# Two halves of the scores swapped at two of seven windows, and a filter stage on quarters of the TensorE array

## The reference, cut to what matters

```python
x = x + conv_ref(_ln_c(x), qkv_w, qkv_b, lepe_w, wo_w, wo_b)
t = _to_tokens(x)
t = t + ffn_ref(_ln_t(t), sigma, phi, M_u, M_phi_plus, M_phi_minus, log_weights, gumbel)

# conv_ref: 49 windows of 64 pixels, the 4 best windows of each
logits = q_win * SCALE @ k_win.T
topk_logit, r_idx = jax.lax.top_k(logits, 4)
kv_sel = kv_pix[arange(N)[:, None, None], r_idx]
attn = softmax(einsum('npqhd,npkhd->nphqk', qh * SCALE, kh))
out = einsum('nphqk,npkhd->npqhd', attn, vh) + lepe          # lepe: 3x3 depthwise of v
out = out @ wo_w + wo_b

# ffn_ref, for each of four branches: filters by FFT of length 4096, then mixed over k and d
U_plus = irfft(rfft(phi) * rfft(u)); U_minus = sgn * irfft(rfft(phi) * rfft(u * sgn))
out = einsum('btkd,k,kde->bte', U_plus, sigma**.25, Mpp) + einsum('btkd,k,kde->bte', U_minus, sigma**.25, Mpm)
out = out + sum(einsum('btd,de->bte', shift(u, i), M_u[i]) for i in range(3))
```

## Time and profile before

| | us |
|---|---|
| time, median of 3 runs | 3991.84 (3982.6 to 4000.59) |
| profiled execution, own time | 3988.77 |
| its span, first to last instruction | 3986.9 |
| PE busy | 3188.3 (80%) |
| DVE busy | 2336.5 (59%) |
| ACT busy | 2164.8 (54%) |
| POOL busy | 1308.3 (33%) |

### The profile page before, as it was taken

The page is one execution under the profiler, slowest core; times in us unless marked ns, Lnnn a source line. Parts: engine busy times, 40 slices in busy tenths (PEclk is TensorE's granted clock), DMA queues, the critical chain, the costliest instruction groups (busy, mean ns, idle before and its releaser), DMA issues. The chain is left out here.

```text
span 3986.9 us, 161803 instructions
## 1 busy us (share of the span) xinstructions
PE 3188.3 (80%) x52286; PEld 2268.0 (57%) x52286; DVE 2336.5 (59%) x3853; ACT 2164.8 (54%) x4973; POOL 1308.3 (33%) x4161
## 2 busy tenths in 40 slices
PE   4418988988888898889888888988888257999955
PEld 1205665666566565656555665656666027888855
DVE  2246777677667666766776676677665282333322
ACT  1106766766676676667666766766787122333310
POOL 1004444445444444544444444445443100000000
PEclk9999999989998899999899999999999578999977
DMA  2423544543454355345434543543322675777779
GB/s 75 130 62 103 141 103 104 138 118 100 112 139 102 91 132 130 97 103 141 110 97 117 133 104 93 139 125 98 86 44 47 105 234 124 143 151 147 152 201 294
DMA packets 819875, 485.10 MB, mean 122 GB/s; under 512 B 561946, under 2 KB 798875, under 8 KB 813883
## 3 DMA queue, kind: packets, MB, share of 16 engines
q1 hardware_dynamic: 756386, 408.10, 41.8%
q10 hardware_dynamic: 62720, 67.46, 6.7%
HBM read 264.58 MB, written 209.19 MB: 119 GB/s over the span
## 5 line engine op out<-in xcount | busy, mean ns | idle before, releaser
L556 POOL COPY Ksel<-Kexp 96x128 int32 x3136 | 961.1, 349 | 1210.0 <-PE ps L1185 1078.8
L920 DVE TENSOR_REDUCE Mx<-ps 128x2 f32<-128x512 f32 x1568 | 1062.7, 687 | 459.6 <-PE ps L1163 452.6
L769 ACT ACTIVATE Pr<-ps 128x1024 f32<-128x1024 f32 x784 | 800.5, 1021 | 772.2 <-PE ps L1185 730.4
L1183 PE MATMUL ps<-Qbd,Ksel 96*128 96x128 bf16 x6272 | 853.2, 226 | 22.7 <-issue 22.2
L689 ACT ACTIVATE Vsel<-Vpx 64x72 f32 x3136 | 815.5, 260 | 94.9 <-DMA Vpx<-v_dram 25.8
L1185 PE MATMUL ps<-MT,each 84*128 84x128 bf16 x6272 | 853.8, 226 | 0.0
L1163 PE MATMUL ps<-Ksel,Qbd 96*128 96x256 bf16 x3136 | 630.7, 284 | 133.0 <-POOL Ksel L556 127.8
L1183 PEld LDWEIGHTS ps<-Qbd,Ksel 96*128 96x128 bf16 x6272 | 634.7, 101 | 97.6 <-issue 89.4
L1185 PEld LDWEIGHTS ps<-MT,each 84*128 84x128 bf16 x6272 | 635.8, 101 | 88.6 <-issue 81.7
L1202 PE MATMUL ps<-Pr,Vsel 128*9 128x64 f32 x25088 | 519.8, 225 | 67.3 <-ACT O L697 43.3
L1202 PEld LDWEIGHTS ps<-Pr,Vsel 128*9 128x9 f32 x25088 | 378.1, 92 | 255.3 <-issue 254.8
(11 more groups left out here) (169 smaller groups left out, 3505.1 us busy)
## 6 DMA issues: line engine op xcount, KB each, us to landing
q_dram<-Pq SPq DMA_DIRECT2D x336, 112.0 KB, 2.1
k_dram<-Pk SPq DMA_DIRECT2D x336, 112.0 KB
Kexp<-k_dram ACTq DMA_DIRECT2D x112, 336.0 KB, 4.3
Qbd<-q_dram SPq DMA_DIRECT2D x224, 168.0 KB, 3.9
Vpx<-v_dram ACTq DMA_DIRECT2D x224, 126.0 KB
s_dram<-S SPq DMA_DIRECT2D x8, 2048.0 KB, 7.1
Sin<-s_dram SPq DMA_DIRECT2D x64, 256.0 KB, 5.1
z_dram<-Zs SPq DMA_DIRECT2D x128, 128.0 KB, 2.4
```

The costliest lines, as they stand in the source:

```text
L556: nc.gpsimd.tensor_copy(dst[:, w, :, k, :], src[:, :, bass.ds(win[k] * (PX // 2), PX // 2)])\
L769: nc.scalar.activation(Pr[k][:].rearrange("q c p h x -> q (c p h x)"), ps[:, ST0 + 2 * k:ST0 + 2 * k + 2, :].rearrange("q a b -> q (a b)") ...
L920: nc.vector.tensor_reduce(Mx[u % 2][:, 2 * half:2 * half + 2, w], ps[:, half, :].rearrange("q (p k) -> q p k", p=2), AX.X, ALU.max).then_i ...
L1183: mm(out, Ksel[u % 2][:, w, p, 2 * c:2 * c + 2, :].rearrange("r k x -> r (k x)"), query(u, w, p), start=True, stop=False)
```

## The change

Two edits that have nothing to do with each other.

In the windows whose scores stand behind a transpose of the maxima (`TURNED`, w = 2 and w = 6 in PE's order), the two halves of the scores change places: bank 1 first, then `weighted`, then bank 0, and the hold for `mt_copied` moves to the latter. DVE takes the two maxima in the same order; the counts that PE and DVE wait for follow by `place`.

In the mixer Mbd loses its zero blocks: [128, 8, 4, 64] in place of [128, 64, 2, 64]. Each half of its rows now holds other output columns, so `choose` computes 2048 elements a row in place of 4096. V is computed for both frequency halves on both halves of the partitions (128 columns in place of 64), Vh is twice as large, and G becomes eight groups of 16 matmuls of 35 rows by 64 columns, each on one quarter of the array, that fill two banks. Two memsets (Mbd on POOL, Vh on DVE) go.

```diff
+TURNED = ((2 + LEAD) % NWIN, (6 + LEAD) % NWIN)
+        def place(n, aw, half):
+            return n * 2 + (half ^ (aw in TURNED)) + 1
+        def halves(aw):
+            return (1, 0) if aw in TURNED else (0, 1)
...
             def row_max(n, u, w, half):
-                hold(dve, "dve", s_ready, n * 2 + half + 1)
+                hold(dve, "dve", s_ready, place(n, w, half))
...
-                        row_max(n, au, aw, 0)
+                        row_max(n, au, aw, halves(aw)[0])
...
-                        row_max(n, au, aw, 1)
+                        row_max(n, au, aw, halves(aw)[1])
...
             def scores(d, n, u, w, half):
-                if half == 0:
+                if half == halves(w)[0]:
                     hold(pe, "pe", k_gathered, n * TOPK + TOPK)
...
-                hold(pe, "pe", max_done, n * 2 + half - 1)
+                hold(pe, "pe", max_done, place(n - 1, (w - 1) % NWIN, half))
...
                     if more:
-                        if w == 2:
-                            hold(pe, "pe", mt_copied, g * 2 + 2)
-                        if w == 6:
-                            hold(pe, "pe", mt_copied, g * 2 + 3)
-                        scores(ad, n, au, aw, 0)
+                        scores(ad, n, au, aw, halves(aw)[0])
                     if w > 0:
                         weighted(g, u, w - 1)
...
                     if more:
-                        scores(ad, n, au, aw, 1)
+                        if w == 2:
+                            hold(pe, "pe", mt_copied, g * 2 + 2)
+                        if w == 6:
+                            hold(pe, "pe", mt_copied, g * 2 + 3)
+                        scores(ad, n, au, aw, halves(aw)[1])
...
-        Mbd = tensor(filters, "Mbd", [128, C, 2, C])
+        Mbd = tensor(filters, "Mbd", [128, 8, 4, C])
...
-                nc.gpsimd.memset(Mbd[:], 0.0).then_inc(cleared, 1)
...
-                    dst = Mbd[rows, :, h, :].rearrange("p e d -> p d e")
+                    dst = Mbd[rows].rearrange("p n j d -> p d n j")
+                    src = raw[rows, i, :].rearrange("p (d n r j) -> p r d n j", n=8, r=2, j=4)[:, h]
...
-            Vh = tensor(ctx, "Vh", [128, 2, NB])
+            Vh = tensor(ctx, "Vh", [128, 2, 2, NB])
...
                     for k in range(2):
-                        mm(ps[0:KAP, I_BANK, NB * k:NB * k + NB], Sf[:, k, :], Fv[:, k, 0:NB], start=True, stop=True)
-                        last = mm(ps[C:C + KAP, I_BANK, NB * k:NB * k + NB], Sf[:, k, :], Fv[:, k, NB:2 * NB],
+                        mm(ps[0:KAP, I_BANK, 128 * k:128 * k + 128], Sf[:, k, :], Fv[:, k, :], start=True, stop=True)
+                        last = mm(ps[C:C + KAP, I_BANK, 128 * k:128 * k + 128], Sf[:, k, :], Fv[:, k, :],
                                   start=True, stop=True)
...
-                    for n in range(16):
-                        hold(pe, "pe", g_dve if n % 2 else g_act, p * 8 + (n // 2 + 1))
+                    for n in range(8):
+                        hold(pe, "pe", g_act, p * 8 + (n + 1))
+                        hold(pe, "pe", g_dve, p * 8 + (n + 1))
                         for e in range(4):
-                            last = mm(ps[:, n % 4, 128 * e:128 * e + 128],
-                                      Mbd[:, 4 * n + e].rearrange("k h d -> k (h d)"),
-                                      Vh[:].rearrange("k a x -> k (a x)"), start=True, stop=True)
-                        last.then_inc(g_mm, 1)
+                            for r in range(2):
+                                rows = slice(C * r, C * r + KAP)
+                                for h in range(2):
+                                    last = mm(ps[C * h:C * h + C, (2 * n + r) % 4, 128 * e:128 * e + 128], Mbd[rows, n, e, :],
+                                              Vh[rows, :, h, :], start=True, stop=True)
+                                if e == 3:
+                                    last.then_inc(g_mm, 1)
```

More of the change, by code:

```diff
@@ L983, in _ @@
             for n in range(LEAD):
-                for half in range(2):
+                for half in halves(n):
                     row_max(n, 0, n, half)
@@ L1165, in scores, with transpose_max @@
                 last.then_inc(s_ready, 1)
-            def transpose_max(g, u, part, n):
+            def transpose_max(g, u, part, n, aw):
                 hold(pe, "pe", m_split, g * 8 + 4 * part + 4)
-                hold(pe, "pe", max_done, n * 2 + 1)
+                hold(pe, "pe", max_done, place(n, aw, 0))
                 nc.tensor.transpose(ps[:, 0, :].bitcast(BF16)[0:NMAX, 0:128],
@@ L1228, in _ @@
             for n in range(LEAD):
-                for half in range(2):
+                for half in halves(n):
                     scores(0, n, 0, n, half)
-            transpose_max(0, 0, 0, LEAD - 1)
+            transpose_max(0, 0, 0, LEAD - 1, LEAD - 1)
             def slot(d, u, first, last):
@@ L1259, in slot @@
                     if w == 2:
-                        transpose_max(g, u, 1, held)
+                        transpose_max(g, u, 1, held, (aw - 1) % NWIN if more else LAST)
                     if w == 6 and not (last and u == UNITS - 1):
-                        transpose_max(g + 1, (u + 1) % UNITS, 0, held)
+                        transpose_max(g + 1, (u + 1) % UNITS, 0, held, (aw - 1) % NWIN if more else LAST)
                     if w == 2 and behind:
@@ L1434, in _ @@
                     sp.dma_start(raw[r + 2 * KPHI:r + KAP], m_u.rearrange("i k d e -> k i (d e)")).then_inc(m_loaded, 16)
-                sp.wait_ge(cleared, 3)
+                sp.wait_ge(cleared, 2)
                 def load(k, p):
@@ L1539, in _ @@
                 step_done(nc.vector.tensor_tensor(wgt[:, :], dif[:, :], z8[:, 0:4], ALU.add))
-                dve.wait_ge(cleared, 4)
+                dve.wait_ge(cleared, 3)
                 dve.wait_ge(sk_step, 2)
@@ L1570, in choose @@
                     rows = slice(C * h, C * h + KAP)
-                    dst = Mbd[rows, :, h, :].rearrange("p e d -> p d e")
+                    dst = Mbd[rows].rearrange("p n j d -> p d n j")
+                    src = raw[rows, i, :].rearrange("p (d n r j) -> p r d n j", n=8, r=2, j=4)[:, h]
                     if i == 0:
-                        step_done(nc.vector.tensor_scalar(dst, raw[rows, 0, :].rearrange("p (d e) -> p d e", e=C), wgt[rows, 0:1], None, ALU.mult))
+                        step_done(nc.vector.tensor_scalar(dst, src, wgt[rows, 0:1], None, ALU.mult))
                     else:
-                        step_done(nc.vector.scalar_tensor_tensor(out=dst, in0=raw[rows, i, :].rearrange("p (d e) -> p d e", e=C), scalar=wgt[rows, i:i + 1],
+                        step_done(nc.vector.scalar_tensor_tensor(out=dst, in0=src, scalar=wgt[rows, i:i + 1],
                                                                  in1=dst, op0=ALU.mult, op1=ALU.add))
@@ L1775, in step @@
                     hold(act, "act", v_mm, p + 1)
-                    copy(Vh[0:KAP].rearrange("k a x -> k (a x)"), ps[0:KAP, I_BANK, 0:128]).then_inc(v_sb, 1)
+                    copy(Vh[0:KAP].rearrange("k a h x -> k (a h x)"), ps[0:KAP, I_BANK, 0:256]).then_inc(v_sb, 1)
                     copy_g(act, "act", copy, g_act, 0, p)
@@ L1792, in _ @@
                 nc.vector.memset(ps[:, Z_BANK:Z_BANK + 2, :], 0.0)
-                nc.vector.memset(Vh[:], 0.0)
                 for n, (s, credit) in enumerate([(g_act, 2), (g_dve, 2), (z_mm, 1), (z_act, 1), (z_dve, 1), (i_mm, 4),
@@ L1801, in step @@
                     hold(dve, "dve", v_mm, p + 1)
-                    copy(Vh[C:C + KAP].rearrange("k a x -> k (a x)"), ps[C:C + KAP, I_BANK, 0:128]).then_inc(v_sb, 1)
+                    copy(Vh[C:C + KAP].rearrange("k a h x -> k (a h x)"), ps[C:C + KAP, I_BANK, 0:256]).then_inc(v_sb, 1)
                     copy_g(dve, "dve", copy, g_dve, 1, p)
```

## The result

The changed kernel takes 3868.95 us (median of 4 runs, 3857.22 to 3878.32), the kernel before 3990.48 on the same chip (4 runs): a ratio of 0.969, 95% interval 0.966 to 0.973. The forecast was 3825 us, with a range of 3780 to 3885.

What follows compares the result with a forecast made beforehand. PE was taken to bound attention and the mixer's second stage, DVE's coefficients the first stage; -92 (attention), -29 and -43 sum to -164 from 3988.8, so 3825 us, range 3780 to 3885 (0.82).

Steps and rivals of the forecast that it cites:

- The wait moved off the scores (-101): Attention: PE does first scores and weighted values while the maxima are copied, so its waits before the scores shrink by 101 us.
- What attention gives back (+9 and +10): Attention: 9 us for a new wait in the following window, 10 us for weighted values still waiting for ACT's copies.
- The new wait of the window behind: Attention: the window after a swapped one waits for bank 0's later maximum, 0.3 us each, 9 us together.
- ACT's copies of O: Attention: the weighted values' wait for these copies, a loop that doesn't shorten, was let take back 10 us.
- The clock in attention (-10): Attention: shorter waits mean fewer drops to half clock, 0.3 us for each of 35 units, 10 us less.
- The first stage (-29): Mixer, first stage: DVE's coefficients halve their elements at the same price by element, 29 us less.
- The second stage (-43): Mixer, second stage: three rounds gain 5.7 us each and 13 gain 2.0 each, 43 us less, bounds +5 and -55.
- I take four at once: Mixer, second stage: G's matmuls run on all four array quarters at once; with its copies G takes 8.5 us a round.
- the wait for Zr of some 2.8: Mixer, second stage: Zr lands when it did, so PE waits some 2.8 us before the inverse; 2.9 of 5.7 us count.
- The failing term: Mixer, second stage: half clock behind the new wait before the inverse, half of the rounds losing 1.7 us.
- the signs that the forecast had named: Second stage: G at 8 to 9 us, a new 2 to 3 us wait for Zr, a round of 28.7 to 30.
- only two quarters at once: Rival, chance 0.12: G in the second stage stays at 14.5 us, the round grows by 0.34, total 3873 us.

Runs made afterwards that it cites:

- Run 3: The changed kernel (both edits), but each of G's quarter matmuls takes all 64 rows, rows 35 to 63 being zeros: 3816.83 us (0.958).
- 4: The changed kernel (both edits, 35 rows in G) plus two unused matmuls of 128 rows on PE between V and G: 3836.74 us (0.963).
- 5: The changed kernel (both edits) plus two unused matmuls between V and G that take 35 rows in place of 128: 3841.2 us (0.963).
- after: The changed kernel with both edits, against the kernel before: 3868.95 us (0.969).

## Why the prediction was right or wrong

**The wait moved off the scores (-101): right.** Counted by place it fell by 107.7 (130.6 to 22.9), and the step at 1630.78 goes as it was told: from transpose to second scores 1.85 us in place of 3.06, so 1.2 where 1.1 was taken.

**What attention gives back (+9 and +10): the right kind, too small, and at another place.** The new wait of the window behind came, with 5.8 us for 9. ACT's copies of O take nothing back (-1.7); the projection does (+44), since DVE's scaling of O waits for sums that come by way of DRAM, and the forecast had no term for that. In all PE's idle time fell by 65 us (2761.3 - 2413.4 = 347.9 to 283.2).

**The clock in attention (-10): too small.** PE's busy time fell by 39 us at the same number of instructions, with the granted clock at 0.98 in place of 0.96. That attention came within 12 us is in part luck, since the two errors cancel: 65 + 39 = 104, forecast 82 + 10 = 92.

**The first stage (-29): right**, -31, by the halved coefficients at 4480 and 2020 ns (4.5 and 1.9 forecast).

**The second stage (-43): the step that failed, +10.** That is outside the bounds of +5 and -55 that the forecast gave it. "I take four at once" held, and so did G's 8.5 us and the wait for Zr of some 2.8: at clock 1.00 they were 8.5 and 2.92. The failing term is the clock's. It was put behind the new wait ahead of the inverse, at 1.7 us in half of the rounds, and at nothing inside G. But G ran mostly at half clock in 14 of 16 rounds, so that it took 12.7 to 13.7 us in most of them and the inverse behind it, in part at half clock too, 5.5 to 6.1 in place of 4.2. So G's price of 8.5 us took for granted a clock that, in before, a busy PE had kept (0.98 in that stage). The missing row would have been one of a stretch of matmuls with few rows behind an idle microsecond, and before had none: the 0.88 us there was followed by matmuls of 128 rows, most of whose coefficients were zeros. Of the signs that the forecast had named, G at 8 to 9 us and a round of 28.7 to 30 did not come; the round took 32.1. Run 3 shows the term alone: with zero rows put back the second stage takes 492.5 us, -37 against the -43 forecast, and its round is 1.7 us shorter than before (31.6 to 29.9), where 2.0 was taken. That the whole time still lies in the stated range is luck as far as this stage goes: the range was wide enough for it, for the sake of other rivals.

**The rivals.** The time of 3869 is near that of "only two quarters at once" (3873), but for another reason: the quarters ran four at once in every round. A time can agree with a wrong mechanism, and only the timeline tells them apart. That rival came by a rule of the Trainium skill ("TensorE: Matmul & The Clock Gate", part 3, What overlaps and what doesn't): weight loads overlap with matmuls in flight only where the row group differs, which made G 14.5 us. The trace does not agree: at clock 1.00 G took 8.5.

What stays open is how idle time and rows add up in the clock: runs 3, 4 and 5 show that either more rows in G or work ahead of it keeps the clock up, not by what measure, and no number of rows between 35 and 64 was tried.

## What to carry to other kernels

Work that is taken out of a matmul, even zeros, can cost the clock: look at the granted clock of the stretch after the change, and if it fell, try filled rows or a throwaway matmul in the idle time ahead before giving the idea up. Look for ready work to put in the place of a wait on the critical engine: here two halves that change places brought some 100 us, and moving the inverse behind half of Uh 52. Ask what is late next, too: here a way through DRAM took some of the gain back. Split such a wait by where it occurs first; here one of two windows held 123.6 of 130.6 us.

## What the runs showed of the hardware

- Four matmuls on four 64x64 quarters of the array, two of them in the same rows, ran at once: 256 records of 272 ns each in 8.1 us busy, 32 ns apart on average. Full-array records of as many columns start 111 ns apart in the kernel before.

```profile
L1854 PE MATMUL mps<-Vh,Mbd 35*64 35x128 f32 x256 | 8.1, 272 | 1.6 <-DVE Vh L1810 1.1 <-DVE Gs L1752 0.3
```

- The granted clock can fall to 0.50 while PE has no idle time: in after 1.92 us into a stretch of matmuls of 35 rows that stood behind 1.12 us of idle time, and for 13.65 us.
- Rows of zeros kept it up: 64 rows in place of 35 in each quarter made G 8.4 us in place of 12.7 to 13.7, and the kernel 52 us faster.
- 1.03 us of useless matmuls in a wait of 1.1 us made the kernel 32 us faster (3868.95 to 3836.74), 27 of them in the second stage.
